# Expert tiles put in an order that lets six of eight batches be normed beside the last four tiles

## The reference

```python
probs = softmax(xt @ gate_w + gate_b)
top_v, top_i = top_k(probs, 2)                       # two of eight experts for each of 4096 tokens
combine = sum(one_hot(top_i, 8) * top_v[..., None], axis=1)
for e in range(8):
    h = gelu(xt @ W1[e] + b1[e]) @ W2[e] + b2[e]     # 256 -> 1024 -> 256
    out = out + combine[:, e:e+1] * h
x = x + layernorm(out, ln2_g, ln2_b)                 # mean and variance of each token
```

## Time and profile before

| | |
|---|---|
| median of 3 runs | 2513.82 us (2511.02 to 2516.73) |
| the profiled execution, its own time | 2516.9 us |
| its span, first to last instruction | 2515.1 us |
| mean granted TensorE clock | 0.936 |
| PE busy, DVE busy, ACT busy, POOL busy | 88%, 52%, 41%, 28% |

### The profile page before, as it was taken

How to read it: one execution, slowest core, us unless ns; L and a number is a source line. 1 busy time by engine, 2 the same in 40 slices (tenths; PEclk the granted TensorE clock), 3 DMA queues, 4 the chain that set the end, 5 groups by cost and what they waited for, 6 DMA issues and landing times. The chain is left out here.

```text
span 2515.1 us, 33628 instructions
## 1 busy us (share of the span) xinstructions
PE 2202.1 (88%) x10760; PEld 1249.3 (50%) x10760; DVE 1306.3 (52%) x3466; ACT 1024.0 (41%) x1837; POOL 710.0 (28%) x718
## 2 busy tenths in 40 slices
PE   6897489994999999999999999999539999999990
PEld 2574256661333333334334344343237888888880
DVE  5456633312777777776777777777272111111115
ACT  2223111110566666565666666656202233322222
POOL 3114223334111001112213334322203333333335
PEclk9998789996999999999999999999769999999995
DMA  4326444425423232222333443342007666666664
GB/s 165 104 100 209 151 145 108 107 48 91 92 57 69 57 70 52 44 61 27 49 44 46 60 60 52 43 52 35 17 10 209 191 177 185 189 184 187 178 190 138
DMA packets 198737, 254.80 MB, mean 101 GB/s; under 512 B 21264, under 2 KB 176912, under 8 KB 196560
## 3 DMA queue, kind: packets, MB, share of 16 engines
q1 hardware_dynamic: 177200, 224.10, 34.8%
q0 software_dynamic: 20544, 28.33, 6.6%
q10 hardware_dynamic: 864, 0.79, 0.3%
HBM read 161.95 MB, written 52.67 MB: 85 GB/s over the span
## 5 line engine op out<-in xcount | busy, mean ns | idle before, releaser
L1787 ACT ACTIVATE att_prob<-att_ps 128x512 f32<-128x512 f32 x1024 | 594.7, 597 | 383.6 <-PE att_ps L1649 197.3
L1632 PE MATMUL att_pm<-att_kstack,att_qstack 96*128 96x512 bf16 x1024 | 402.4, 394 | 27.8 <-DMA att_qstack<-att_q 24.2
L1922 DVE CUSTOM_DVE_ANT_0 att_junk<-att_pm,bias 128x512 bf16<-128x512 f32 x512 | 343.5, 688 | 158.6 <-PE att_pm L1632 157.6
L1918 DVE TENSOR_REDUCE att_tops<-att_pm 128x1 f32<-128x512 f32 x512 | 340.2, 682 | 120.4 <-PE att_pm L1632 117.6
L1646 PE MATMUL att_ps<-att_qstack,att_kstack 99*128 99x512 bf16 x1024 | 392.7, 385 | 4.6 <-ACT att_prob L1787 3.0
L1199 PE MATMUL exL_po<-exL_w,exL_hid 128*128 128x256 f32 x1696 | 379.5, 382 | 17.7 <-DVE exL_ys L1266 8.9
L1183 PE MATMUL exL_ph<-exL_xgT,exL_w 128*128 128x256 f32 (+2 forms) x1504 | 387.5, 413 | 5.7 <-ACT exL_hid L1216 3.0
L1216 ACT ACTIVATE exL_hid<-exL_ph,exL_b 128x256 f32<-128x256 f32 (+2 forms) x376 | 186.8, 501 | 438.9 <-PE exL_ph L1183 422.1
L1199 PEld LDWEIGHTS exL_po<-exL_w,exL_hid 128*128 128x128 f32 x1696 | 317.9, 190 | 70.7 <-issue 14.5
L1183 PEld LDWEIGHTS exL_ph<-exL_xgT,exL_w 128*128 128x128 f32 x1504 | 268.8, 191 | 109.7 <-issue 59.6
L1149 POOL DMA_INDIRECT sum<-exL_ys,exL_put x106 | 174.2, 1644 | 421.7 <-DVE exL_ys L1266 250.7
(11 more groups left out here) (311 smaller groups left out, 2408.7 us busy)
## 6 DMA issues: line engine op xcount, KB each, us to landing
exL_w<-in_L_W SPq DMA_DIRECT2D x94, 1024.0 KB, 5.3
att_qstack<-att_q SPq DMA_DIRECT2D x186, 128.0 KB, 5.8
kstack<-pick_k SPq DMA_DIRECT2D x48, 256.0 KB, 3.1
att_kstack<-kstack SPq DMA_DIRECT2D x16, 768.0 KB, 7.8
att_kstack<-att_k SPq DMA_DIRECT2D x96, 128.0 KB, 4.6
exL_b<-in_L_b SPq DMA_DIRECT2D x47, 128.0 KB, 5.3
values<-pick_vals SPq DMA_DIRECT2D x8, 574.0 KB, 4.7
att_vals<-values SPq DMA_DIRECT2D x8, 574.0 KB, 4.0
```

Source lines behind the costliest of these rows:

```text
L1632: pe.matmul(pm[i % TOPS][:], stack["q"][par][0:KR, h, t * P:(t + 1) * P], stack["k"][par][0:KR, h, :], start=True, stop=True).then_inc(s[" ...
L1787: act.activation(prob[i % PROBS][:], ps[i % 2][:], ACT.Exp, scale=SCALE).then_inc(s["p_ready"], 1)
L1918: ins = dve.tensor_reduce(tops[g % 2][:, t, j:j + 1], pm[i % TOPS][:], AX.X, ALU.max)
L1922: ins = dve.tensor_tensor_reduce(junk[:, i % TOPS, :], pm[i % TOPS][:], G["bias"][0][:, t, :], 1.0, -BIG / 2, ALU.add, ALU.max, tops[g % 2 ...
```

## The change

The 39 tiles are kept, but they run in a new order, `ORDER`: tiles 0 to 23 in 12 loop pairs, then 15 written out: 24, 25, 35, 26, 27, 36, 28, 29, 37, 30, 38, 31, 32, 33, 34. The half tiles 35 to 38 now stand between whole ones. `top_experts` gives each expert first the tiles that hold its tokens of batches 0 to 5 (`started`; at most `BEGUN` = 31 of these over all experts), and then the rest. So the tiles 31 to 34, the last four, hold only tokens of batches 6 and 7. The stage `finish` is gone. Its work is in `experts`, under new names (`exL_y`, `exL_ystats`, `exL_ymv`, `exL_yrstd`, `exL_ynbias`). In what follows `CLOSED` is 35, and "the tile at 35" is the one at position 35 of the order, the first of the last four.

```diff
+SPLIT = 6 * CB
+BEGUN = (SPLIT * P * TOPK + E * (TILE - 1)) // TILE
+LOOPED = 24
+ORDER = tile_order()
+CLOSED = ORDER.index(BEGUN)
@@ experts, SP
+                    sp.dma_start(gain[:], a["L1_ln2_g"].broadcast_to([P, D])).then_inc(gain_in, 16)
+                    def load_and_read(t, slot, pair):
+                        load(t, slot, pair)
+                        if isinstance(t, int) and t == CLOSED + 1:
+                            sp.wait_ge(added, begins(CLOSED) * 16)
+                            for b in range(0, 3):
+                                read(b)
+                        if isinstance(t, int) and t == CLOSED + 2:
+                            for b in range(3, 6):
+                                read(b)
+                    run(sp, load_and_read, 2)
+                    for b in range(0, 4):
+                        write(b)
+                    sp.wait_ge(added, begins(tiles) * 16)
+                    read(6)
+                    read(7)
+                    for b in range(4, B):
+                        write(b)
@@ POOL, before the scatters of a tile
+                    if not early and isinstance(t, int) and t == CLOSED + 1:
+                        rstds(0, 3)
+                    if not early and isinstance(t, int) and t == CLOSED + 2:
+                        rstds(3, 6)
@@ ACT, behind a tile's Gelus: norm(0..2) at CLOSED + 1, norm(3..5) at CLOSED + 2; norm(6), norm(7) at the end
@@ DVE
+                        if isinstance(t, int) and t == LOOPED:
+                            add_shift(slice(NC // 2, NC))
+                        if isinstance(t, int) and t == CLOSED:
+                            dve.wait_ge(gain_in, past(16))
+                            for b in range(0, 3):
+                                stats(b)
+                        if isinstance(t, int) and t == CLOSED + 1:
+                            for b in range(3, 6):
+                                stats(b)
+                            add_norm(0)
+                        if isinstance(t, int) and t == CLOSED + 2:
+                            for b in range(1, 4):
+                                add_norm(b)
+                    run(dve, tile_and_rows)
+                    add_norm(4)
+                    add_norm(5)
+                    stats(6)
+                    stats(7)
+                    add_norm(6)
+                    add_norm(7)
```

More of the change, by code:

```diff
@@ L1216, in tile, with norm @@
                         act.activation(hid[:, f, 0:n * P], ph[f % 2][:, 0:n * P], gelu, bias=b1[slot][:, f:f + 1]).then_inc(hid_ready, 1)
-                run(act, tile)
+                def norm(b):
+                    act.wait_ge(y_rstd, past(b + 1))
+                    for c in range(b * CB, (b + 1) * CB):
+                        ins = act.activation(Y[:, c, :], Y[:, c, :], ACT.Identity, bias=ynbias[:, c:c + 1],
+                                             scale=yrstd[:, c:c + 1])
+                        if c % 2:
+                            ins.then_inc(y_normed, 1)
@@ new lines, in _ @@
+                chain(dve.tensor_tensor(full[:], to(so_far, [P, E, N // TILE], 2), to(steps[:], [P, E, N // TILE], 1),
+                                        ALU.is_gt))
+                chain(dve.tensor_reduce(started[:], full[:], AX.X, ALU.add))
+                chain(dve.tensor_tensor(started[:], started[:], whole[:], ALU.min))
+                chain(dve.tensor_tensor(cross[:], G["lower"][:], to(started[:], [P, E, E], 1), ALU.mult))
+                chain(dve.tensor_reduce(first[:], cross[:], AX.X, ALU.add))
@@ new lines, in _ @@
+                chain(dve.tensor_tensor(last[:], first[:], started[:], ALU.add))
+                chain(dve.tensor_tensor(last2[:], whole[:], started[:], ALU.subtract))
+                chain(dve.tensor_tensor(cross[:], G["lower"][:], to(last2[:], [P, E, E], 1), ALU.mult))
+                chain(dve.tensor_reduce(first2[:], cross[:], AX.X, ALU.add))
+                chain(dve.tensor_scalar(first2[:], first2[:], last[:, E - 1:E], None, ALU.add))
+                chain(dve.tensor_tensor(last2[:], last2[:], first2[:], ALU.add))
@@ L2170, in _ @@
-                chain(dve.tensor_tensor(past_end[:, WHOLE:, :], to(ended[0:1, :], [1, HALVES, E], 1),
+                chain(dve.tensor_scalar(started[:], started[:], float(TILE), None, ALU.mult))
+                for n, ends in enumerate((last, last2)):
+                    chain(dve.tensor_tensor(past_end[:, 0:WHOLE, n * E:(n + 1) * E],
+                                            to(ends[0:1, :], [1, WHOLE, E], 1),
+                                            to(G["lane"][0:1, 0:WHOLE], [1, WHOLE, E], 2), ALU.is_le))
@@ L2322, in build @@
         lists(nc, G, "L1", 1, TOPK * NC, COLS, False)
[L2323 to L2324 removed]
+        experts(nc, G, a, "L1", ACT.Gelu, out=out)
 def kernel(**inputs):
```

240 lines of the change are left out of this document (123 added, 117 removed).

## The result

| | before | after |
|---|---|---|
| median of the runs | 2512.74 us (4 runs, 2511.02 to 2516.73) | 2483.43 us (4 runs, 2479.56 to 2485.51) |
| the profiled execution, its own time | 2516.9 us | 2485.5 us |
| its span | 2515.1 us | 2483.8 us |
| mean granted TensorE clock | 0.936 | 0.944 |

The ratio is 0.9883, with a 95% interval of 0.9869 to 0.9896: the changed kernel is faster by 29 us. The forecast was 2481.7.

A forecast was written before the change was run, and what follows sets the result against it. PE was taken to bound the tiles, busy 401.60 of 410 us in the looped ones. Terms -38.0 + 1.8 - 2.2 + 5.2 + 1.1 = -32.1 us, from 2513.8 to 2481.7 us; range 2475 to 2490.

The forecast's parts named there:

- tail: From the last matmul's end to the span's end: 63.9 us shrinks to 25.9, so -38.0, between 32.5 and 39.
- norms in the tile at 37: ACT's 12 norms end at 17.6 us, past the next tile's first Gelu at 15.8: PE stands 1.8 us (0.7 to 2.9).
- loop and order: Eight tiles leave the loop as four pairs, -2.2 us; half tiles between whole ones cost nothing.
- ranking: Ahead of the tiles, `top_experts` gains 18 instructions in its chain on DVE: +5.2 us.
- semaphores: The expert stage raises 17 more ahead of those the first gather waits for, 0.062 us each: +1.1 us.
- E + 8.4: In the tail, 8.4 us after the last matmul's end (E), the last scatter has landed and batch 6 can be read.
- upper bound for the scatter behind DVE: If the last scatter finds no gap before eight DVE instructions end, it waits 3.2 us; 0.6 was taken.
- POOL is free at P + 8.4: POOL can begin its chain for 12 columns 8.4 us after the start of the tile at 36 (P).
- The half tiles did not stall PE: Rival: POOL is late by up to 2 us for each of the four half tiles, +8, 2490 us; chance 0.05.
- The reads were in time: Rival: late reads make DVE's statistics delay the next tile's copy and PE; slower, 2514 us and more; chance 0.02.
- The merged stage alone: Rival: only the stage is merged, all eight batches' norms end behind the last scatter: -7.3 + 4.1, 2511 us; chance 0.02.
- the first rival: Side work holds PE and the tail: power at 3.1, second norm group paying 2, scatter and read at bounds; 2490 us; chance 0.15.

The follow-up runs named there:

- The three comparisons of the unchanged kernel: The changed kernel without further edit, measured three times against the kernel before: 2483.43 us (ratio 0.9883), 2487.69 us (0.9905) and 2480.79 us (0.9869).
- experiment 5: Against the changed kernel, SP waits for one more scatter, the first of the tile at 35, before the three reads: 2489.84 us, ratio 0.9908.
- experiments 5 and 7: The 7: new order with old closing stage, 2513.47 us; new order and merged stage, nothing normed ahead, 2502.47; kernel before with 12 loop turns, 2511.2.

## Why the prediction was right, point by point

The terms, against the first profile of the change:

| term | forecast | measured |
|---|---|---|
| tail | -38.0 | -39.0 |
| norms in the tile at 37 | +1.8 | +6.2 (+2.7 and +3.0 in the others) |
| loop and order | -2.2 | -2.2 |
| ranking | +5.2 | +5.4 |
| semaphores | +1.1 | +1.0 |
| lists, not forecast | 0 | +0.7 |
| start of the ranking stage, before the change | 0 | -3.3 |
| sum | -32.1 | -31.2 |

The sum of the spans' difference, 31.3 us, is met. But that is luck: the norms cost 4.4 more than forecast in this execution, and against that the tail gained 1.0 more and 3.3 us came from ahead of the change. The three comparisons of the unchanged kernel give 29, 24 and 33 us by their ratios; the forecast of 32.1 lies among them.

- **The tail: right, by its steps.** Three of its steps were pessimistic. The first read was set at E + 8.4 and came at E + 6.65: the scatter was not held by DVE, and it landed 2.2 us after its end, not 3.0. The second batch's statistics followed the first's with no gap, as taken. Against that the last batch's chain on POOL was slowed by DVE's additions (an instruction of 0.24 took 0.68), and the norms of batch 7 started at E + 17.7, where I had 18.2. (The upper bound for the scatter behind DVE was 6.3 - 3.2 = 3.1 and not 3.2, which changes nothing.)
- **DVE against POOL: near the lower bound.** In the tail the scatter took 1.55 us beside additions of 0.7 us back to back; one tile earlier, beside the same additions, 2.04. Beside the 4.42 us shift of `x` at the tile at 24 it took 3.81 and ended 1.4 us behind the shift. So a long DVE instruction holds a scatter to its end; for these short ones the price was 0 to 0.5 us, where the forecast had 0.6 and, at the bound, 2.6 more. The Trainium skill (page SBUF — State Buffer, section "SBUF: two separate sides" and, in it, "Who interferes with whom") has VectorE and GpSimd lock each other out of a shared port for a whole instruction, for a VectorE instruction with two SBUF inputs only against a GpSimd one that reads SBUF, and it infers that a `tensor_tensor` does not hold up the writing of a DMA's descriptors. The 3.81 here and the 5.01 in the earlier trace rows against 1.58, both beside a `tensor_tensor` with two SBUF inputs, differ from that inference.
- **The norms: the right place, mis-sized.** The gap came where I put it, ended by ACT, and there was none in the tile at 38. The step that failed is "POOL is free at P + 8.4". It took the row of a tile without reads. With the reads and the weight load behind them in flight POOL was free at P + 11.0, because the scatter's landing took 5.8 us in place of 3.0. (The reads themselves were forecast at P - 8.2 and issued at P - 5.0, and were still in time.) The chain took 3.4 where I had 3.0 (its power 2.31, forecast 2.1), and the norms 6.0 where I had 6.2. The second part of the miss is the lower clock behind the wait of 4.34 us, some 1.6 us (7.04 against 5.45), which I did not cost at all. In the two other profiles the landing was at 3.9 and 4.1, the clock stayed, and the term is 2.7 and 3.0, at the edge of the bounds given (0.7 to 2.9).
- **Rivals.** The half tiles did not stall PE (8.63 and 8.64 each). The reads were in time in the change (statistics ready at 2414.72, POOL free for them at 2419.5); in experiment 5, where they come later, POOL waits for the statistics and PE for POOL, so late reads reach PE through the norms before DVE's copy is late. The merged stage alone was given 2511; it measured 2502. The read comes 9.1 sooner behind E (15.7 to 6.7), and from the first statistics to the end it is 38.3 us in place of 44.2. That second part I had not counted; POOL no longer multiplies every other batch (2.35 us each), which is the likely reason, but no run tests it alone. Of the first rival only the part in the tile at 37 came.

## What to carry to other kernels

Side work that is hidden beside a full engine is placed by when it starts, not by how long it takes: 6.9 us of extra ACT work directly behind a tile's Gelus cost nothing, and 6.0 us that started 7 us later in the tile held PE for 4.3. When transfers are moved next to other transfers, take no landing time from a stretch without them, and look for what waits on a landing in a queue: here a scatter, two gathers and a list stood between the landing and a chain of four small instructions that everything waited for; putting it ahead of the gathers took the wait in the tile at 37 away. And keep a stall of TensorE short, if it can't be avoided: behind the three longest here, 3.81 to 5.25 us, the matmuls were slow too.

## What the hardware showed that I had not expected

- The landing of a scatter of 128 rows of 1 KB beside three 512 KB reads and a 1 MB weight load issued 1.3 us behind them: 5.8 us of waiting when the reads were issued 3.5 us before it, 3.9 to 4.4 at 5.0 to 5.4 us, and 2.8 to 3.0 when neither was still under way (experiments 5 and 7).
- Waits of PE of 2.45, 2.46 and 2.76 us left the granted clock at 1.00; those of 3.81, 4.34 and 5.25 were followed by 24 matmuls at 7.0 to 8.3 us in place of 5.45. The Trainium skill (page TensorE: Matmul & The Clock Gate, "Part 1: The HAM clock gate") has the clock fall to half after idle time; the traces agree, and show that this is paid inside a tile too.
- The power on POOL costs by width: 1.05 us for 4 columns and 2.31 for 12, so by an estimate from these two 0.16 us for a column and 0.4 for the instruction.
- What stays open: single runs of the changed kernel lie up to 16 us apart (2475.7 to 2491.9), more than the 9 us of the kernel before (2507.5 to 2516.7), and more than the varying wait explains. In the traces the tiles begin at 1890.9 to 1899.7 although the code ahead of them is the same in all the changed kernels that norm inside the stage. Nearly all of it is there at the first instruction of `top_experts` (1809.0 to 1818.0): from there to the first matmul it is 81.2 to 81.9 us in each. So the difference arises ahead of the part that was changed; what makes it was not tried.
